# A Mamba scan on two vector engines: a quarter of the products of dt, x and B and three bias additions move from DVE to Pool

## The reference, cut to what matters

```python
dA  = exp(dt_t[..., None] * A)
dBx = dt_t[..., None] * B_t[:, None, :] * x_t[..., None]
h   = dA * h + dBx
y_t = sum(h * C_t[:, None, :], axis=-1)
```

## Time and profile before

| | |
|---|---|
| median of 3 runs | 3942.16 us (3936.2 to 3948.75) |
| the profiled execution, its own time | 3951.12 us |
| its span, first to last instruction | 3949.3 us |
| PE busy | 3210.4 us, 81% |
| DVE busy | 3004.6 us, 76% |
| ACT busy | 1953.3 us, 49% |
| Pool busy | 650.5 us, 16% |
| granted clock of TensorE, mean | 0.933 |

### The profile page before, as it was taken

One profiled execution on the slowest core, in us unless ns is written; L12 is line 12 of the kernel. 1 busy time (PEld: TensorE's weight loads), 2 busy tenths in 40 slices (PEclk: granted clock), 3 DMA queues, 4 the chain that ended last, 5 costly groups with the idle time before them and its releaser, 6 DMA issues.

```text
span 3949.3 us, 57618 instructions
## 1 busy us (share of the span) xinstructions
PE 3210.4 (81%) x21250; PEld 2199.1 (56%) x21250; DVE 3004.6 (76%) x6496; ACT 1953.3 (49%) x4513; POOL 650.5 (16%) x516
## 2 busy tenths in 40 slices
PE   2468988788797888978888897988879888887877
PEld 1245656556464655646556564655646565564655
DVE  5678796877878688796868879687887868778632
ACT  2336455564545546455554645555464554645422
POOL 0303030120303012040210304021030301204000
PEclk8679999999999989999999999989999998999987
DMA  6526171532716235181523517153361614427100
GB/s 213 131 56 174 50 197 63 157 119 89 203 50 184 77 123 153 54 238 49 155 95 116 171 50 225 52 159 99 96 196 50 197 63 146 130 74 215 55 31 16
DMA packets 205833, 470.84 MB, mean 119 GB/s; under 512 B 23856, under 2 KB 43952, under 8 KB 190832
## 3 DMA queue, kind: packets, MB, share of 16 engines
q1 hardware_dynamic: 205552, 467.17, 39.2%
HBM read 446.11 MB, written 20.97 MB: 118 GB/s over the span
## 4 chain that ended last, share of the span: by engine, by line
PE 41%; DVE 34%; ACT 9%; issue 8%; DMA 6%; SPq 1%; POOL 0%; DVEq 0%; ACTq 0%
DVE region_x L1449 7%; PE ps L864 6%; DMA region_x<-rows_of_dt 5%; DVE region_x L1432 5%; PE ps L633 4%; PE ps L824 3%; PE ps L810 3%; PE ps L497 3%; ACT region_y L1148 3%; PE ps L845 3%; PE ps L614 2%; DVE nm L1486 2%; PE ps L645 2%; DVE x_stats L1284 2%; PE ps L569 2%
## 5 line engine op out<-in xcount | busy, mean ns | idle before, releaser
L1227 POOL TENSOR_TENSOR region_x<-region_x 128x512 f32<-128x512 f32 x512 | 650.3, 1270 | 2982.6 <-DVE region_x L1449 2982.6
L1028 ACT ACTIVATE ps<-region_x,aneg 128x255 f32<-128x255 f32 x1024 | 443.1, 470 | 446.2 <-DVE region_x L1449 431.3
L1449 DVE TENSOR_TENSOR_SCAN region_x<-ps,region_x 128x512 f32<-128x512 f32 x512 | 622.9, 1217 | 16.0 <-ACT ps L1028 15.1
L1432 DVE TENSOR_TENSOR region_x<-region_x,ps 128x512 f32<-128x512 f32 x512 | 343.1, 671 | 49.2 <-DMA region_x<-rows_of_dt 46.2
L864 PE MATMUL ps<-xTy,wide 128*128 128x256 f32 x1280 | 307.1, 395 | 0.0
L1148 ACT ACTIVATE region_y<-ps,rmax 128x256 f32<-128x256 f32 x512 | 235.7, 500 | 140.9 <-DVE rmax L1591 140.9
L1499 DVE SCALAR_TENSOR_TENSOR region_x<-region_x,cntk 128x512 f32<-128x512 f32 x256 | 167.0, 689 | 156.2 <-ACT region_x L1066 156.2
L864 PEld LDWEIGHTS ps<-xTy,wide 128*128 128x128 f32 x1280 | 244.5, 196 | 42.3 <-issue 10.1
L561 PE MATMUL ps<-region_x,sely 128*32 128x512 f32 x1024 | 157.5, 691 | 121.6 <-POOL region_x L1227 121.3
L614 PE MATMUL ps<-region_y 64*128 64x256 f32 x1024 | 176.9, 485 | 91.5 <-DVE VP L1572 37.4
L633 PE MATMUL ps<-region_y 64*128 64x256 f32 x1024 | 173.1, 464 | 95.9 <-ACT region_y L1066 49.5
(11 more groups left out here) (246 smaller groups left out, 6491.9 us busy)
## 6 DMA issues: line engine op xcount, KB each, us to landing
region_x<-rows_of_dt SPq DMA_DIRECT2D x1024, 256.0 KB, 5.3
wide<-in_wgate SPq DMA_DIRECT2D x16, 1280.0 KB, 8.4
wide<-in_wup SPq DMA_DIRECT2D x16, 1280.0 KB, 11.0
down<-in_wmoe SPq DMA_DIRECT2D x16, 1280.0 KB, 5.6
wide<-in_wq SPq DMA_DIRECT2D x16, 1024.0 KB, 4.8
wide<-in_wk SPq DMA_DIRECT2D x16, 1024.0 KB, 6.9
wide<-in_wv SPq DMA_DIRECT2D x16, 1024.0 KB, 8.9
down<-in_wo SPq DMA_DIRECT2D x16, 1024.0 KB, 7.8
```

The source lines that it names most:

```text
L1028: last = f(ps[:, 1 + 2 * (k % 2), m * T + 1:(m + 1) * T], dt_rep[k % SLOTS][:, m, 1:T], ACT.Exp, scale=aneg[:, k, m:m + 1])
L1227: nc.gpsimd.tensor_tensor(hbuf[k % HSLOTS], hbuf[k % HSLOTS], csb.unsqueeze(1).to_broadcast([P, 2, T]), ALU.mult).then_inc(hc_ready, 1)
L1432: tt_(hbuf[k % HSLOTS], dtx_rep[k % SLOTS], ps[:, 2, 0:T].unsqueeze(1).to_broadcast([P, 2, T]), ALU.mult).then_inc(dbx, 1)
L1449: nc.vector.tensor_tensor_scan(flat(hbuf[k % HSLOTS]), ps[:, 1 + 2 * (k % 2), :], flat(hbuf[k % HSLOTS]), 0.0, ALU.mult, ALU.add).then_inc ...
```

## The change

- **Products.** Product k with k mod 4 = 3 (8 of 32) is left out on DVE and made by Pool, from `dtx_rep[3]` and a copy of B in SBUF. Its tile goes to the same place in `hbuf`.
- **The copy of B.** ACT copies PSUM bank 2 to `bsb`, the place of `dtr`, after the logarithm of the first half of dt. DVE still reads B from PSUM, but its first product now waits for the copy's semaphore.
- **Pool's list.** Pool makes product 3 before its first multiplication by C, and product k+3 ahead of the multiplication of unit k for k = 4, 8, ..., 28. Product 3 waits for the stores of dt; product k+3 waits for `y_ps` of at least max(1, k/4-1) groups.
- **Waits that follow.** DVE's scan of such a unit waits for `dbx_pool`; SP's load of slot 3 of `dtx_rep` waits for `dbx_pool`.
- **Biases.** Pool adds `ob1` to sequence i-1 ahead of scan i, then after scan i `ob2` to sequence i-1 and `fb2` to sequence i. The first waits for stream y's first transpose, the second for the second transpose, the third for the first quantised tile. DVE has a wait for `bias_added` at each of the three places.
- **Order.** All four patterns of `ORDER` are written anew. On DVE stream y starts 7 pieces earlier in x's count; y's first query piece stands after the softplus of the second half of dt and no longer before it; most pieces of the cross-attention and of the experts move by one or two places. On PE, between group 0 and group 1 stand score pieces 2 to 8 of the self-attention (before: 2 and 4), and between 1 and 2 pieces 10 to 14.
- Semaphores that nobody waits for are no longer made.

```diff
     def first_half(i):
-                    if k >= SLOTS:
-                        sp.wait_ge(dbx, at(i, UNITS, k - SLOTS + 1))
+                    if k >= SLOTS and k % SLOTS == SLOTS - 1:
+                        sp.wait_ge(dbx_pool, at(i, UNITS // 4, k // 4))
+                    elif k >= SLOTS:
+                        sp.wait_ge(dbx, at(i, 24, k // 4 * 3 - 3 + k % 4 + 1))
...
     # ACT, in mamba(); called after the first half's Ln
+                def b_copy():
+                    act.wait_ge(xdbl, at(i, 3, 3))
+                    f(bsb, ps[:, 2, 0:T], ACT.Copy).then_inc(b_sb, 1)
...
     # Pool
+            def add_row(i, row):
+                x = xh[:, i % 2]
+                nc.gpsimd.tensor_tensor(x, x, row[:].unsqueeze(1).to_broadcast([P, TT, D]), ALU.add).then_inc(bias_added, 1)
+            def self_bias(i):
+                pool.wait_ge(Y.xT_ps, at(i, 3, 1))
+                add_row(i, W["ob1"])
+            def cross_bias(i):
+                pool.wait_ge(Y.x_ready, at(i, 2, 1))
+                pool.wait_ge(Y.xT_ps, at(i, 3, 2))
+                add_row(i, W["ob2"])
+            def ffn_bias(i):
+                pool.wait_ge(f_q, at(i, 4, 1))
+                add_row(i, W["fb2"])
             for i in range(B):
+                if i:
+                    self_bias(i - 1)
                 pool.wait_ge(c_sb, i + 1)
+                def product(k):
+                    if k == 3:
+                        pool.wait_ge(b_sb, i + 1)
+                        pool.wait_ge(dtx_done, at(i, 2, 2))
+                        for stored_rows in dt_stored:
+                            pool.wait_ge(stored_rows, at(i, 32, 32))
+                    else:
+                        pool.wait_ge(y_ps, at(i, 8, max(1, k // 4 - 1)))
+                    pool.wait_ge(rep_dtx[3], at(i, 128, 16 * (k // SLOTS + 1)))
+                    nc.gpsimd.tensor_tensor(hbuf[k % HSLOTS], dtx_rep[3], bsb.unsqueeze(1).to_broadcast([P, 2, T]),
+                                            ALU.mult).then_inc(dbx_pool, 1)
+                product(3)
                 for k in range(UNITS):
+                    if k % 4 == 0 and k:
+                        product(k + 3)
                     pool.wait_ge(h_ready, at(i, UNITS, k + 1))
                     ...
+                if i:
+                    cross_bias(i - 1)
+                ffn_bias(i)
...
     # DVE
                 def product(k):
+                    if k % 4 == 3:
+                        return
...
-                v.wait_ge(xdbl, at(i, 3, 3))
+                v.wait_ge(b_sb, i + 1)
...
-                    v.wait_ge(dbx, at(i, UNITS, k + 1))
+                    if k % 4 == 3:
+                        v.wait_ge(dbx_pool, at(i, UNITS // 4, k // 4 + 1))
+                    else:
+                        v.wait_ge(dbx, at(i, 24, k // 4 * 3 + k % 4 + 1))
...
-                c.link(tt_(x, x, W["fb2"][:].unsqueeze(1).to_broadcast([P, TT, D]), ALU.add))
+                v.wait_ge(bias_added, at(i, 3, 1))      # in ffn_end
-                c.link(tt_(x, x, W["ob1"][:]...))   ->  v.wait_ge(bias_added, at(i, 3, 2))
-                c.link(tt_(x, x, W["ob2"][:]...))   ->  v.wait_ge(bias_added, at(i, 3, 3))
```

More of the change, by code:

```diff
@@ L90, in close @@
         assert self.n == self.per, f"steps per sequence: {self.n}, stated {self.per}"
-X_STEPS = 70
+X_STEPS = 69
 END_STEPS = 5
 DIGIT_STEPS = 8
-Y_STEPS = 38
+Y_STEPS = 36
 A_STEPS = 7
@@ L195, in build @@
         dtr = in_x(11536, (T,))
+        bsb = dtr
         xin = in_x(3328, (M, PAD))
@@ L269, in build @@
         batch_done = sem("batch_done")
+        b_sb, dbx_pool, bias_added = sem("b_sb"), sem("dbx_pool"), sem("bias_added")
         class Attention:
@@ L283, in __init__ @@
                     self.rinv = sb(tag + "_rinv", (P, TT, 4, 4))
+                    self.oT_ps, self.norm = sem(tag + "_oT_ps"), sem(tag + "_norm")
+                    self.on_ps, self.oT = sem(tag + "_on_ps"), sem(tag + "_oT")
+                else:
+                    self.kevac, self.rsum = sem(tag + "_kevac"), sem(tag + "_rsum")
+                    self.ln, self.shift = sem(tag + "_ln"), sem(tag + "_shift")
+                if masked:
+                    self.weighed = sem(tag + "_weighed")
                 self.proj = sem(tag + "_proj")
@@ L385, in first_half @@
                 sp.wait_ge(decay_ready, at(i, UNITS, UNITS))
-                sp.wait_ge(dbx, at(i, UNITS, UNITS))
+                sp.wait_ge(dbx, at(i, 24, 24))
+                sp.wait_ge(dbx_pool, at(i, UNITS // 4, UNITS // 4))
                 for row, name in ((fb1, "fb1"), (ln2g, "ln2g"), (ln2b, "ln2b")):
@@ L1018, in mamba @@
                     f(sp_l[:, ms], sp_e[:, ms], ACT.Ln, bias=onec[:, 0:1]).then_inc(dt_ln, 1)
+                    if half == 0:
+                        b_copy()
                 for k in range(UNITS):
@@ L1228, in _ @@
                                             csb.unsqueeze(1).to_broadcast([P, 2, T]), ALU.mult).then_inc(hc_ready, 1)
+                if i:
+                    cross_bias(i - 1)
+                ffn_bias(i)
+            self_bias(B - 1)
+            cross_bias(B - 1)
         @block.vector
@@ L1576, in self_attention @@
                 yield from narrow_attention(i, c, att1, self_values)
-                c.link(tt_(x, x, W["ob1"][:].unsqueeze(1).to_broadcast([P, TT, D]), ALU.add))
+                v.wait_ge(bias_added, at(i, 3, 2))
                 yield from residual_norm(Y, i, c, 1, 1, bank(4), Y.x_ready)
@@ L1602, in cross_attention @@
                 yield
-                c.link(tt_(x, x, W["ob2"][:].unsqueeze(1).to_broadcast([P, TT, D]), ALU.add))
+                v.wait_ge(bias_added, at(i, 3, 3))
                 yield from residual_norm(Y, i, c, 2, 2, bank(5), Y.x_ready)
```

14 lines of the change are left out of this document (4 added, 10 removed), and 15 rows, old and new, of the table ORDER.

## The result

The changed kernel takes 4027.15 us (median of 4 runs, 4024.91 to 4035.53), the kernel before 3945.45 beside it (4 runs, 3936.2 to 3953.3). The ratio is 1.0212 [1.0184, 1.024]: slower by 82 us, where I forecast 40 us faster, and outside my range. The profiled execution's own time is 4027.62 us.

The account below looks back on a forecast made before the run. PE and DVE share the bound, DVE pacing the scan and the feed-forward's end. Gross 6.07 us a sequence less costs, 0.6 given back, left 2.47, 40 us for 16: 3942 - 40 = 3902 us, range 3875 to 3930 (8 in 10: 3860 to 3965).

Parts of the forecast that it names:

- term 10: New orders of all pieces: same instructions, most moved one or two places; taken as 0, bounds -2 and +2 us a sequence.
- Terms 1 and 2: DVE relieved of eight products in the scan, 4.64 us, and of ob1 and fb2, 1.43 us, per sequence.
- term 3: ob2 taken off DVE where DVE has slack: counted as nothing, 0.7 us if that cover were gone.
- term 7: Pool's additions of fb2 and ob1 block DVE instructions beside them: 0.45 us each, 0.9 us lost a sequence.
- Term 4: First groups of the scan: Pool's product 7 waits for group 0, delaying DVE twice by 0.6 us, 1.2 a sequence.
- Term 5: Scan-only stretches: four units cost Pool 6.35 us against DVE's 6.26, so Pool sets the pace; 0.4 us lost a sequence.
- Term 6: Port shared by Pool and DVE: tiny DVE steps blocked by Pool once more per sequence, 1.2 us lost, bounds 0 and 4.8.
- Term 8: DMAs in the scan: SP's later slot 3 load and the shorter scan add 0.5 us of waiting, bounds 0 and 3.
- Term 9: ACT's copy of B: about 0.38 us where ACT was idle, before DVE's first product; costs nothing.
- C: Rival: PE waits for Pool's later groups, up to 8.9 us against 6.07 gained; slower, 3987 us; 0.19 including slower Pool products.
- B: Rival: DMAs set the scan's length, ceiling 253 GB/s, floor 74.9 us; no change, 3942 us; chance 0.16.
- A: Rival: the gross time comes out in full, 6.07 us a sequence; 3845 us, or 3865 with locks; chance 0.17.

Follow-up runs that it names:

- b_neworder: The kernel before with the new order and nothing else, none of the changed work on Pool: 4061.09 us, ratio 1.0291.
- the middle: The kernel before with the new order only from the attention weights to the end of the feed-forward, 112 table loads kept: 4000.95 us, ratio 1.0115.
- h_pre2: h_scan plus the new order from dt to the first scan, SP's new pattern, fb2 added earlier and product 7 not waiting for group 0: 3937.25 us.
- h_early7: h_scan with Pool's product 7 no longer waiting for PE's group 0: 3940.95 us, ratio 0.9989.
- h_scan: The changed kernel with all of Pool's work, but the new order only inside the scan and the old order elsewhere: 3945.92 us, ratio 0.999.
- h_fh: h_scan with Pool adding fb2 when the feed-forward's first half is dequantised, not at the first quantised tile: 3942.63 us, ratio 0.9991.
- h_pre2_prod: h_pre2 with the three bias additions back on DVE, only the eight products on Pool: 3942.69 us, ratio 0.9991.

## Why the prediction was wrong, by its steps

**The step that failed is term 10**: "Most pieces move by one or two places, with the same instructions. I take 0, bounds -2 and +2 us." It measured 114 us / 16 = 7.1 us a sequence (`b_neworder`), three and a half times the bound, and alone it turns the sign. The words "with the same instructions" are wrong for ACT: 58 table loads came in. The diff showed the order of the pieces, and the trace of the kernel before had the price of a load, 1.28 us, and each engine's idle time by stretch; I worked out neither. Two parts of it are shown: the normalisation within the convolution (58 us alone) and the middle (53 us alone). They come near the 114 together, but taking the first out of the changed kernel returns only 18, so the parts don't add up in a simple way.

The rule that I should have weighed is in the Trainium skill, page "ScalarE: Activation LUTs", section "Table sets: the hidden batching unit": group activations by table set. The same page of the Trainium skill, section "What ACT_TABLE_LOAD costs", prices a load at about 1283 ns and a further 1380 of draining. The rows agree with the first (1283 ns in each of 170); of the second they show nothing, since two loads in a row take 2.57 us and the next activation begins at 976.39, at once.

**Terms 1 and 2, the gross gain.** The counts came as forecast: 384 products on DVE, 128 on Pool, 48 additions. DVE's busy time fell by 83.0 us; removed were, on my account, (4.64 + 0.71 + 0.72) x 16 = 97 and 11 of ob2 (term 3). The locks of term 7 give 22 back, which leaves 86.

**All of Pool's work, net.** I forecast 40 us. It measured 34 us in the new order, 38.5 in `h_pre2`'s, -14 in the old. The first two are near the sum; none of the runs splits it into all its terms, and a sum that is right proves no term.

**Term 4, the first groups.** Seen at its place: DVE's scan of unit 7 waits for the product, and the product for PE's group.

```profile
1026.28 1.27 POOL L1267 TENSOR_TENSOR region_x<-region_x 128x512 f32<-128x512 f32 x1 [4.18 <-PE ps L563]
1027.58 1.22 DVE L1507 TENSOR_TENSOR_SCAN region_x<-ps,region_x 128x512 f32<-128x512 f32 x1 [0.59 <-POOL region_x L1267]
...
1034.67 0.69 DVE L1487 TENSOR_TENSOR region_x<-region_x,ps 128x512 f32<-128x512 f32 x1 [1.33 <-PE ps L563]
```

The scan waits 0.59 us, as worked out (0.6); DVE's wait for groups of PE is 21.2 us in all over L1487, 1.3 a sequence, against 0.6. I gave half of it back. `h_early7`, which removes the first wait, differs from `h_scan` by less than the interval.

**Term 5, Pool as pace-setter.** Hardly borne out. Pool is busy 47.65 of the 72.56 us of the scan above. In a short run of units it does work without a gap:

```profile
1027.50 4.97 POOL L1275 TENSOR_TENSOR region_x<-region_x 128x512 f32<-128x512 f32 x4
```

Four in a row took 4.97 us, 1.23 apart; the product starts 4.91 us after the first of them, and the next four start 1.24 us after the product. So five take 6.15 us, under DVE's 6.26, and not 6.35.

**Term 6, the lock on tiny steps.** Sized at 1.2 us a sequence, measured about 0.2. The mean of the 48 is 495 ns, before 510; of the 48 of the line ahead of it, L1349, five took 0.29 to 0.95 us instead of 0.16, 2.8 us more in all.

```profile
L1350 DVE SCALAR_TENSOR_TENSOR y_nt<-y_nt,y_rstd 128x2 f32<-128x2 f32 x48 | 23.8, 495 | 1.7
```

**Term 7, the lock on the additions.** Sized at 0.9, measured 1.4 a sequence. Beside Pool's addition of fb2, which runs from 936.52 for 1.31 us, the second step of a quantised tile takes 1.24 us instead of 0.29; beside ob1's, a half of the softplus 0.85 instead of 0.42:

```profile
935.82 0.29 DVE L1383 TENSOR_SCALAR region_x<-region_x 128x256 f32<-128x256 f32 x1
936.52 1.31 POOL L1235 TENSOR_TENSOR xh<-xh,fb 128x512 f32<-128x512 f32 x1 [92.15 <-DVE region_x L1384]
936.74 1.24 DVE L1383 TENSOR_SCALAR region_x<-region_x 128x256 f32<-128x256 f32 x1
...
992.25 0.85 DVE L1459 TENSOR_SCALAR region_x<-region_x 128x512 f32<-128x512 f32 x1
996.13 0.42 DVE L1459 TENSOR_SCALAR region_x<-region_x 128x512 f32<-128x512 f32 x1
```

In sum over the 32 instructions of each kind that is 15.2 and 6.4 us more than before, 0.95 and 0.4 a sequence. This is the rule that I weighed at 2.5, of the Trainium skill's page "SBUF — State Buffer", section "SBUF: two separate sides". The mechanism is as stated: the two steps ended 0.15 and 0.28 us after Pool's addition; the full price isn't reached because DVE meets only part of each addition. `h_fh` removes the first block whole, with no measurable effect on the time.

**Term 8, DMAs.** DVE's wait for `rows_of_dt` rose from 46.2 us to 81.2, 2.2 a sequence against 0.5. Most of the rise, 1.8, is at products 0 and 1, at the scan's start (0.6 and 2.4 us a sequence); from product 2 on the wait is 2.3 and 2.7.

```profile
DVE region_x L1487 <- DMA region_x<-rows_of_dt: 81.2, 95, 2.8
...
PE ps L563 <- POOL region_x L1275: 68.8, 12, 22.9
```

**Term 9** is as forecast: the first product waits for DMAs, not for ACT's copy.

**The rivals.** C had the sign and not the cause. It said that PE would wait over 200 us for Pool; the row above has 68.8, less than the 121.3 before. Its 3987 is no hit. B is refuted: the tails above moved data at 394 and 410 GB/s, far over the 253 I named as a possible ceiling, and over the 358 that the prediction has from the Trainium skill. (Its floor of 74.9 us is of a window of 79 us; it can't be held against the 72.56 us from the first scan to the last, which was 75.02 before.) A's scan of 6 us less came nowhere; the shortest is 3.3 less. The mean granted clock fell from 0.933 to 0.930, within the bound that I set; by stretch it moved by up to 0.12, and the bound on the mean hid that.

**What stays open.** Why the parts of the order don't add up (the granted clock has a share in it), why the middle costs what it does, how much of a seam's price is its loads and how much the moved piece, what the biases are worth (`h_pre2` and `h_pre2_prod` are 5.4 us apart and their intervals overlap), and what each of terms 4 to 8 took by itself.
